# Rotary attention: one projection of q or k for four heads in a slot, shared scaling of the probabilities, and another order of the slot

## What is computed

```python
def _rope(x, theta):
    ...
    x1, x2 = (x[..., 0::2], x[..., 1::2])
    return jnp.concatenate([x1 * cos - x2 * sin, x1 * sin + x2 * cos], axis=-1)
...
q = (xn @ q_w + q_b).reshape(b, s, H, HD).transpose(0, 2, 1, 3)
k = (xn @ k_w + k_b).reshape(b, s, H, HD).transpose(0, 2, 1, 3)
v = (xn @ v_w + v_b).reshape(b, s, H, HD).transpose(0, 2, 1, 3)
q = _rope(q, theta)
k = _rope(k, theta)
scores = jnp.einsum('bhqd,bhkd->bhqk', q, k) * scale
scores = jnp.where(causal, scores, -jnp.inf)
attn = jax.nn.softmax(scores, axis=-1)
ctx = jnp.einsum('bhqk,bhkd->bhqd', attn, v)
attn_out = ctx @ o_w + o_b + xn
```

## Time and profile before

| | |
|---|---|
| median of 3 runs | 1773.41 us (1769.02 to 1774.05) |
| profiled execution | 1769.51 us, its span 1767.5 us |
| PE busy | 1551.0 us, 88% of the span |
| DVE, ACT, POOL busy | 1113.3, 931.6 and 555.9 us |
| granted PE clock, mean | 0.937 of full speed |
| rotary stage | 1100 to 1499 us |

### The profile page before, as it was taken

The page is one execution under the profiler, slowest core; times in us unless marked ns, Lnnn a source line. Parts: engine busy times, 40 slices in busy tenths (PEclk is TensorE's granted clock), DMA queues, the critical chain, the costliest instruction groups (busy, mean ns, idle before and its releaser), DMA issues. The chain is left out here.

```text
span 1767.5 us, 29904 instructions
## 1 busy us (share of the span) xinstructions
PE 1551.0 (88%) x11045; PEld 847.0 (48%) x11045; DVE 1113.3 (63%) x2537; ACT 931.6 (53%) x2028; POOL 555.9 (31%) x690
## 2 busy tenths in 40 slices
PE   1677686699999999999999997899999997599999
PEld 1344343244454444454545443566666675244444
DVE  4755442477878686878787783566566654355554
ACT  1323233176777777776777676355555554243343
POOL 4010101121121203030303000688788885133331
PEclk9978787599999999999999999999999999699998
DMA  4222210703233323223132220000000000000001
GB/s 101 70 55 55 55 37 18 141 16 98 48 98 48 99 48 99 48 88 57 70 56 62 61 33 6 4 1 1 1 1 1 1 1 1 10 20 20 22 19 37
DMA packets 88422, 75.35 MB, mean 43 GB/s; under 512 B 24725, under 2 KB 78389, under 8 KB 87349
## 3 DMA queue, kind: packets, MB, share of 16 engines
q1 hardware_dynamic: 88276, 73.44, 18.9%
HBM read 42.73 MB, written 30.42 MB: 41 GB/s over the span
## 5 line engine op out<-in xcount | busy, mean ns | idle before, releaser
L1145 DVE TENSOR_REDUCE b_chunk_max<-psum 128x1 f32<-128x400 f32 (+1 forms) x1024 | 540.9, 569 | 176.7 <-PE psum L1359 170.6
L1283 ACT ACTIVATE b_prob<-psum 128x512 f32<-128x512 f32 (+1 forms) x832 | 451.2, 594 | 180.7 <-PE psum L1398 178.9
L1359 PE MATMUL psum<-k_stack,q_stack 128*128 128x400 bf16 (+1 forms) x1024 | 285.4, 343 | 21.0 <-DMA k_stack<-b_k_scratch 17.9
L1368 PE MATMUL psum<-b_prob,b_v_aug 128*32 128x256 f32 (+1 forms) x3328 | 265.9, 391 | 1.7 <-ACT b_prob L1283 0.4
L1398 PE MATMUL psum<-q_stack,k_stack 128*128 128x256 bf16 (+1 forms) x1664 | 253.0, 275 | 0.4 <-DMA q_stack<-b_mparts 0.4
L1398 PEld LDWEIGHTS psum<-q_stack,k_stack 128*128 128x128 bf16 (+1 forms) x1664 | 146.3, 99 | 117.9 <-ACT b_prob L1283 68.8
L1557 POOL TENSOR_SCALAR c_prob<-c_prob,c_rec 128x128 f32<-128x128 f32 (+1 forms) x256 | 191.9, 767 | 8.9 <-POOL c_kT L1566 8.3
L2036 DVE TENSOR_TENSOR e_hg<-e_gl,e_gate 128x512 f32<-128x512 f32 x128 | 123.3, 979 | 113.2 <-PE psum L2051 75.5
L1640 DVE SCALAR_TENSOR_TENSOR c_turned<-psum,c_bias,c_tab 128x256 f32<-128x256 f32 x256 | 106.1, 476 | 112.0 <-PE psum L1773 112.0
L1675 ACT ACTIVATE c_prob<-psum,c_mneg 128x128 f32<-128x128 f32 (+1 forms) x256 | 104.1, 419 | 136.7 <-DVE c_mneg L1617 136.7
L1359 PEld LDWEIGHTS psum<-k_stack,q_stack 128*128 128x128 bf16 x1024 | 99.7, 98 | 128.6 <-DVE b_chunk_max L1145 95.5
(11 more groups left out here) (213 smaller groups left out, 1971.0 us busy)
## 6 DMA issues: line engine op xcount, KB each, us to landing
k_stack<-b_k_scratch SPq DMA_DIRECT2D x32, 600.4 KB, 10.5
b_k_scratch<-b_kparts SPq DMA_DIRECT2D x7, 1200.8 KB, 4.4
b_k_scratch<-b_kparts SPq DMA_DIRECT2D x7, 800.5 KB, 6.3
b_ctx<-in_ctx SPq DMA_DIRECT2D x8, 576.0 KB
e_w<-in_L_ffn_re_w SPq DMA_DIRECT2D x62, 64.0 KB, 1.8
a_scratch<-a_parts SPq DMA_DIRECT2D x16, 192.0 KB, 2.2
k_stack<-a_scratch SPq DMA_DIRECT2D x16, 192.0 KB, 4.7
q_stack<-b_q_scratch SPq DMA_DIRECT2D x32, 96.0 KB, 2.2
```

Source lines behind the costliest of these rows:

```text
L1145: nc.vector.tensor_reduce(out=chunk_max[:, half, q, column4(hh), c:c + 1], in_=max_bank(v)[:, 0:w], axis=AX.X, op=ALU.max).then_inc(max_do ...
L1283: nc.scalar.activation(prob[0:k, buf, par * 2 * T:(par + 1) * 2 * T], st_bank(v, par)[0:k, :], ACT.Exp, scale=HD ** -0.5).then_inc(exp_don ...
L1359: nc.tensor.matmul(max_bank(T_.now("unit"))[:, 0:hi - lo], queries_of(qst, h, slice(q * P, q * P + P)), keys_of(kst, h, slice(lo, hi)), st ...
L1368: last = nc.tensor.matmul(pv[32 * hh:32 * hh + 32, :], v_aug[0:k, kt, g * GH + hh, :], prob[0:k, buf, c:c + T], start=(kt == 0), stop=(kt ...
```

## The change

The weights of q and k come ordered from the host, so that a matrix of 128 columns holds the even parts of four heads and another the odd parts. A slot now projects one of q (even slots) and k (odd slots) for four heads, with two matmuls instead of four. DVE makes four products of it as before, POOL two different sums: the first halves of the turned heads are written in place (the same subtraction into two units of `qT` or `kT`, of which half the rows are then overwritten), the second halves go into `c_second`, and SP places them with four transfers of 32 partitions. Scores follow four slots behind instead of two, turning five, values six, and the drain has eight slots.

The probabilities are scaled by two engines: DVE takes the narrow part (128 columns of each head), POOL the wide one (256), both one slot before the turning. On POOL the scaling stands ahead of the sums and powers. On DVE it stands ahead of the maxima, and the products follow the maxima directly, ahead of norms and items. On PE the projections stand behind the scores. The items move: v in slots 2, 3 and twice in 7, o in 6, `finish` in 7. `order_weights`, the second pair of weight tables, most loads of biases and two products for the table of sines are gone.

```diff
@@ -222,9 +222,9 @@
...
-        self.w1, self.w2 = sb("c_w1", [P, 2, CH * CD]), sb("c_w2", [P, 2, CH * CD])
+        self.w = sb("c_w", [P, 2, UN // 2, 2, P])
         self.tab = sb("c_tab", [P, 2, 2, T])
-        self.bias, self.theta = sb("c_bias", [P, 2, 2, UN]), sb("c_theta", [P, 1])
+        self.bias, self.theta = sb("c_bias", [P, 2, UN // 2, 2]), sb("c_theta", [P, 1])
@@ -1437,9 +1418,9 @@
...
-C_ITEMS = {1: [("v", 0)], 2: [("v", 1)], 5: [("o", 0)], 6: [("v", 2)], 7: [("v", 3)]}
+C_ITEMS = {2: [("v", 0)], 3: [("v", 1)], 6: [("o", 0)], 7: [("v", 2), ("v", 3)]}
 C_PREV = (("o", 0),)
-SCORES_LAG, NORM_LAG, TURN_LAG, VALUES_LAG = 2, 3, 4, 5
+SCORES_LAG, TURN_LAG, VALUES_LAG = 4, 5, 6
 PB = 4
@@ -1516,12 +1499,19 @@
...
         @block.sync
         def _(sp):
             experts_pre.load(sp)
+            for n in range(B * UN):
+                m, u, buf = n % 2, n % UN // 2 * 2, n % 2
+                sp.wait_ge(turned_ready, n + 1)
+                for pos in range(4):
+                    to = 32 * (pos ^ 1)
+                    sp.dma_start((qT, kT)[m][to:to + 32, u + pos % 2, :], second[32 * pos:32 * pos + 32, buf, :])\
+                        .then_inc(placed[m], 16)
         @block.gpsimd
         def _(pool):
@@ -1545,27 +1535,35 @@
             def slot(i, n, first, drain, ahead):
                 u = c_unit(n, 0, first, drain)
+                w = c_unit(n, TURN_LAG, first, drain)
+                if w is not None:
+                    pool.wait_ge(rec_ready, T_.up("weigh"))
+                    for hh in range(2):
+                        ins = nc.gpsimd.tensor_scalar(prob[:, w % PB, hh, P:3 * P], prob[:, w % PB, hh, P:3 * P],
+                                                      rec[:, w % PB, hh, 1:2], None, ALU.mult)
+                    ins.then_inc(wide_weighed, 1)
+                if u is not None:
+                    v = T_.up("unit")
+                    pool.wait_ge(terms_ready, v)
+                    m, g, t4 = u % 2, u // 2 * 2, terms[:, u % 2]
+                    if v > UN:
+                        pool.wait_ge(s_full, (v - 1) // 2 * 2 + 2 - UN)
+                    if v > 2:
+                        pool.wait_ge(placed[m], 64 * ((v - 1) // 2))
+                    nc.gpsimd.tensor_tensor(second[:, m, :], t4[:, 2, :], t4[:, 3, :], ALU.add).then_inc(own_pool, 1)
+                    pool.wait_ge(own_pool, T_.up("own_pool"))
+                    for j in range(2):
+                        nc.gpsimd.tensor_tensor((qT, kT)[m][:, g + j, :], t4[:, 0, :], t4[:, 1, :], ALU.subtract)\
+                            .then_inc((own_pool, turned_ready)[j], 1)
+                        if j == 0:
+                            pool.wait_ge(own_pool, T_.up("own_pool"))
+                    pool.wait_ge(turned_ready, v)
                 if ("o", 0) in c_items(n, first, drain):
                     power()
                 ahead()
-                w = c_unit(n, NORM_LAG, first, drain)
-                if w is not None:
-                    pool.wait_ge(rec_ready, T_.up("weigh"))
-                    pool.sem_inc(passed, 1)
-                    for hh in range(2):
-                        for lo, hi, q in ((0, P, 0), (P, 3 * P, 1)):
-                            ins = nc.gpsimd.tensor_scalar(prob[:, w % PB, hh, lo:hi], prob[:, w % PB, hh, lo:hi],
-                                                          rec[:, w % PB, hh, q:q + 1], None, ALU.mult)
-                    ins.then_inc(weighed, 1)
-                if u is not None:
-                    pool.wait_ge(terms_ready, T_.up("unit"))
-                    par = u % 2
-                    nc.gpsimd.tensor_tensor(qT[:, u, :], turned[:, par, 0, 0, :], turned[:, par, 0, 1, :], ALU.add)\
-                        .then_inc(own_pool, 1)
-                    pool.wait_ge(own_pool, T_.up("own_pool"))
-                    nc.gpsimd.tensor_tensor(kT[:, u, :], turned[:, par, 1, 0, :], turned[:, par, 1, 1, :], ALU.add)\
-                        .then_inc(turned_ready, 1)
-                    pool.wait_ge(turned_ready, T_.now("unit"))
             program(pool, T_, norm, lambda: None, slot)
         @block.vector
@@ -1609,6 +1607,16 @@
...
+                u = c_unit(n, TURN_LAG, first, drain)
+                if u is not None:
+                    dve.wait_ge(exp_done, T_.up("weigh"))
+                    nc.vector.reciprocal(rec[:, u % PB].rearrange("p h q -> p (h q)"),
+                                         total[:, u % PB].rearrange("p h q -> p (h q)")).then_inc(rec_ready, 1)
+                    dve.wait_ge(rec_ready, T_.now("weigh"))
+                    for hh in range(2):
+                        ins = nc.vector.tensor_scalar(prob[:, u % PB, hh, 0:P], prob[:, u % PB, hh, 0:P],
+                                                      rec[:, u % PB, hh, 0:1], None, ALU.mult)
+                    ins.then_inc(weighed, 1)
@@ -1616,32 +1624,26 @@
...
-                u = c_unit(n, NORM_LAG, first, drain)
+                u = c_unit(n, 0, first, drain)
                 if u is not None:
-                    dve.wait_ge(exp_done, T_.up("weigh"))
-                    nc.vector.reciprocal(rec[:, u % PB].rearrange("p h q -> p (h q)"), total[:, u % PB].rearrange("p h q -> p (h q)"))\
-                        .then_inc(rec_ready, 1)
+                    v = T_.up("unit")
+                    dve.wait_ge(proj_full, v)
+                    wait(dve, turned_ready, T_.now("unit", 2))
+                    m, bank = u % 2, (q_bank, k_bank)[u % 2]
+                    for dst, (half, wave) in enumerate(((0, 0), (1, 1), (0, 1), (1, 0))):
+                        ins = nc.vector.scalar_tensor_tensor(out=terms[:, m, dst, :], in0=bank[:, half * T:(half + 1) * T],
+                                                             scalar=bias[:, m, u // 2, half:half + 1], in1=tab[:, m, wave, :],
+                                                             op0=ALU.add, op1=ALU.mult)
+                    ins.then_inc(terms_ready, 1)
                 ahead()
                 items = c_items(n, first, drain)
                 if ("o", 0) in items:
                     item(*items.pop(0), B - 1 if drain else i)
-                if n == 6 and not first:
+                if n == 7 and not first:
                     finish(B - 1 if drain else i)
                 for it in items:
                     item(*it, None)
-                u = c_unit(n, 0, first, drain)
-                if u is not None:
-                    v = T_.up("unit")
-                    dve.wait_ge(proj_full, v)
-                    wait(dve, turned_ready, T_.now("unit", 2))
-                    for m, bank in enumerate((q_bank, k_bank)):
-                        for w in range(2):
-                            ins = nc.vector.scalar_tensor_tensor(out=turned[:, u % 2, m, w, :], in0=bank[:, w * T:(w + 1) * T],
-                                                                 scalar=bias[:, m, w, u:u + 1], in1=tab[:, m, w, :],
-                                                                 op0=ALU.add, op1=ALU.mult)
-                    ins.then_inc(terms_ready, 1)
             program(dve, T_, norm, lambda: T_.up("item"), slot)
         @block.scalar
@@ -1724,7 +1726,9 @@
...
-                    pe.wait_ge(turned_ready, T_.up("scores"))
+                    quads = (T_.up("scores") + 1) // 2
+                    pe.wait_ge(placed[0], 64 * quads)
+                    pe.wait_ge(placed[1], 64 * quads)
                     wait(pe, exp_done, T_.now("scores", 1))
@@ -1735,6 +1739,18 @@
...
+                u = c_unit(n, 0, first, drain)
+                if u is not None:
+                    T_.up("unit")
+                    if n == 0:
+                        pe.wait_ge(item_free, T_.now("item"))
+                    wait(pe, terms_ready, T_.now("unit", 2))
+                    bank = (q_bank, k_bank)[u % 2]
+                    for half in range(2):
+                        last = nc.tensor.matmul(bank[:, half * T:(half + 1) * T], qkw[:, u % 2, u // 2, half, :], xT[:],
+                                                start=True, stop=True)
+                    last.then_inc(proj_full, 1)
@@ -1755,24 +1771,13 @@
...
+                    pe.wait_ge(wide_weighed, T_.now("turn"))
                     wait(pe, probT_ready, T_.now("turn", 1))
                     for hh in range(2):
                         for k in range(3):
                             last = nc.tensor.transpose(psum[:, 4 + hh, k * P:(k + 1) * P], prob[:, u % PB, hh, k * P:(k + 1) * P],
                                                        t["ident"][:])
                     last.then_inc(tp_full, 1)
-                u = c_unit(n, 0, first, drain)
-                if u is not None:
-                    T_.up("unit")
-                    if n == 0:
-                        pe.wait_ge(item_free, T_.now("item"))
-                    wait(pe, terms_ready, T_.now("unit", 1))
-                    for m, bank in enumerate((q_bank, k_bank)):
```

(38 more changed lines are left out.)

44 lines of the change are left out of this document (18 added, 26 removed).

## The result

| | before | after |
|---|---|---|
| median (20 runs each, one chip) | 1772.14 us | 1776.93 us |
| ratio to before | 1 | 1.0025 (95%: 1.0013 to 1.0036) |
| span of the profiled execution | 1767.5 us | 1769.8 us |
| busy PE over the whole span | 1551.0 us | 1502.7 us |

The kernel is 4 to 5 us slower, a quarter of a per cent. First the windows of after. The first row answers to the earlier trace rows; the others are the granted clock behind three waits in the stage.

A forecast was written before the change was run, and what follows sets the result against it. PE set the pace before, POOL's loop would after. Middle batches +2, first -6, last and drain +9.5 give +5.5 us; the clock adds nothing to 3; from the median, 1773.4 + 5.6 = 1779, range 1748 to 1799.

The forecast's parts named there:

- Forecast A: Rotary stage: POOL's loop takes the place of the projections as the bound, 1768 to 1790 us, 46 in 100.
- The placement: One middle batch scheduled by hand, slot by slot: 47.6 us against 47.3, +2 over six batches.
- a plain slot falls not to 3.6 but to 4.6: Slots without items: sums, scalings, turning, scores, maxima and products loop in 9.15 us per two slots, so nothing is won.
- the 56: Ceiling of the gain in us: PE's projections save 0.9 a slot over 64 slots, if nothing else held PE.
- The pair on DVE: DVE's two 128x128 scalings a slot, taken at 1.1 us because POOL works beside nearly each pair.
- The norm of slot 2: The norm's step in slot 2, estimated at 2.2 us from the same kinds of small instructions.
- Landing: SP's four transfers a slot arrive 4.4 us behind POOL's last sum, priced at nothing as they are due three slots later.
- The clock: PE's granted clock may fall behind waits in slots 4 and 0: nothing to 3 us added, and no gain.
- B's decider: DVE in slots 3 and 0 starts its maxima less than 1.5 us after the scores are done.
- B: Faster: slots overlap better than placed by hand, 1755 to 1765 us, down to 1745, 30 in 100.
- C: Slower: clock falls each batch or scaling pairs wait for POOL, 12 to 28 us in all, 1790 to 1805, 18 in 100.
- D: Slower: SP's transfers come late and slots 4 and 6 wait, 1 us a batch and more, about 1790, 6 in 100.

The follow-up runs named there:

- two waits filled: After, with two idle matmuls (1.0 us together) on PE ahead of the turning in slots 0 and 4: 1769.03 us, ratio 0.9996.
- the two kernels that relieve it: After with the second equal subtraction moved to DVE, 1777.13 us; and after with all four scalings on DVE, 1774.11 us.
- half of the projections in the old order: The kernel before, with the second projection pass of q and of k left out behind the first two units: 1746.35 us, ratio 0.9864.
- a lag of three: After, with scores three slots behind their projections instead of four, and everything behind them one slot earlier: 1784.71 us, ratio 1.0070.
- projection-first kernel: After, with PE projecting ahead of the scores and DVE multiplying ahead of the maxima: 1781.16 us, ratio 1.0049.
- the norm's move: After, with stages 2 and 3 of the next norm moved from slots 2 and 3 to slot 6, on POOL too: 1766.14 us, ratio 0.9977.
- the finish's cut: On top of norm in slot 6 and second subtraction on DVE: finish writes an_all directly, its additions come in slot 1 of the next batch; 1752.48 us.
- norm-and-sum kernel: After, with norm stages 2 and 3 in slot 6 and the second equal subtraction on DVE: 1756.63 us, ratio 0.9932.

## Why the prediction was right, point by point

**The outcome.** Forecast A was the case: 1776.93 against 1779, in the stage +6.7 against +5.5. The first batch took 36.4 (34.6 predicted), the middle ones 47.2 (47.6), last batch and drain 71.4 (69.9). The sum came out closer than its terms, which is luck: they are off by +1.8, -2.4 and +1.5. So in part is the 47.2. The placement has no fall of the clock in it, and without falls (two waits filled) the six middle batches take 278.4 where 285.6 were placed; the falls, priced outside the placement, gave 4.8 of this back. The first batch is long in its slots 0 to 2 (5.2, 6.0, 7.7 for 4.15, 5.0, 7.0), where the first scores take 1.65 for 0.93; the clock read 0.81 in it, in the first batch of before 0.91. That the clock is all of it is not shown.

**The loop.** Seven of eight slots in the table are within 0.4 of the placement, the eighth is the one in which the clock fell (in the batches with the fall in slot 1, slots 2 and 3 are off by 0.9 and 1.0), and PE waits before turning in slots 0, 1, 3 and 4 as placed. That the loop over POOL is one of the bounds is shown by all scalings on POOL (+34) and by slot 1 in the two kernels that relieve it. But the step "a plain slot falls not to 3.6 but to 4.6" named one loop where there are two: with POOL's opened, DVE's order holds the slot at 5.2, and with all scalings on DVE the sum stays. Slots 5 and 7, the plain ones, came out at 4.2, on the other loop (scores, maxima, exp, scores again), when the clock held.

**Where the 56 went.** 32 were never there: alone, the saving gives 24. The rest of the change then costs 24 + 4.4, about 29. In the profiles the middle batches are 17 longer than with half of the projections in the old order (283.2 against 266.0), the end 13 (71.4 against 58.3), the first batch 1 shorter.

**Terms that were off.** The pair on DVE, 1.1 predicted, took 0.49 to 0.97 and mostly 0.5 to 0.7; slot 0 is shorter by 0.4. The norm of slot 2, 2.2 predicted, took 2.9 (1292.84 to 1295.71). In slot 3 these two errors cancel: the maxima start 2.3 behind the scores, exactly as placed, by luck. Of the finish, 2.9 to 3.0 predicted, 3.2 came. Landing, 4.4 predicted, was 4.2 at the start of the stage (1109.57 to 1113.81), and at a lag of three no more than 3.6 to 3.8 in most slots and 5.2 in the longest; at a lag of four it costs nothing, as priced. PE's busy time fell by 43, not 50. The clock was put at nothing to 3; taking its falls out is worth 5.

**The shared port.** The scalings beside POOL's scaling were not stopped: 0.70 for the pair, with POOL's 1.84 begun 0.14 behind it, where the shortest pairs take 0.5. One sum beside POOL's subtraction was: L1592 took 0.90 and ended 0.28 behind POOL's end at 1278.84, where it takes 0.43 in the projection-first kernel with POOL idle. The copy before it (L1591, a scaling of 128x256 by 1.0) took 0.77 beside the first of POOL's subtractions and 0.29 in the kernel before with POOL idle at its start, so a scaling can be held as well:

```profile
1277.42 0.77 DVE L1591 TENSOR_SCALAR an_all<-an_cur 128x256 f32<-128x256 f32 x1
```

The rule of the Trainium skill (SBUF — State Buffer, the part on the shared port pair), by which the later one stands for all of the other, agrees with the sum and the copy and not with the pair.

**The rivals.** B's decider, maxima less than 1.5 behind the scores' end (1.3 after their start) in slots 3 and 0, came out by half: 1.0 in slot 3 (1296.33), 2.3 in slot 0 (1280.34). B's gains lie there all the same: the norm's move gives 8.5, the finish's cut 4 to 8. C's clock did fall, in one slot of most batches, behind waits of 1.9 to 2.1, at a price of 5 and not of 12 to 28; the stage's clock read 0.95, above C's 0.93. The Trainium skill (TensorE: Matmul & The Clock Gate, the second failure mode) has idle spells send the clock back: the trace agrees in kind, but not that each such spell does it, as the norm-and-sum kernel waits 1.93 in slot 0 of five middle batches and keeps 1.00. D is out: without transfers the time is the same.

## What to carry to other kernels

When the busiest engine is relieved, price the saving alone first (here 24 of a nominal 56), then place a whole period by hand: the placement came out within 1% of the measured batch, and within 2% of one without a fall of the clock. Where two loops nearly tie, relieving either shows little; look at the slots one by one and find what stands in both, which here was the norm. And compare batches with the same granted clock: of the 8 us between two kernels here, half was falls of the clock in the profiles. An engine's steps that are due at no fixed time belong beside the longest work of another engine. In the o slot of after DVE stands idle for 1.9 us before the sum of o and for 2.7 behind its norm:

```profile
1316.66 0.42 DVE L1583 TENSOR_TENSOR c_o<-psum,an_all 128x256 f32<-128x256 f32 x1 [1.92 <-PE psum L1715]
...
1322.05 0.42 DVE L1624 TENSOR_REDUCE c_mneg<-psum 128x2 f32<-128x256 f32 x1 [2.71 <-PE psum L1739]
```
